# One attention-and-experts kernel: the shift row stored in row order, the first routing block's sums computed inside the last head, band loads moved ahead in the routing queue

## The reference

```python
x = x + attn(layernorm(x)); x = x + ffn(layernorm(x))
# attn: A = softmax(Q K^T / 4);  out = (0.6 * A + 0.4 * L) @ V;  out @ Wo.T + bo
#       L: a band, non-zero for |q - t| <= 3, rows normalised
# ffn:  rh = gelu(x @ rW1 + rb1);  p = softmax(rh @ rW2 + rb2);  top 2 of 4 experts
#       out = sum over the two experts e of p_e * (gelu(x @ We1[e] + be1[e]) @ We2[e] + be2[e])
```

## Time and profile before

| | us |
|---|---|
| median of 3 runs | 1982.28 |
| lowest, highest | 1981.71, 1989.45 |
| the profiled execution | 1984.26 |
| its span | 1982.5 |
| PE busy | 1915.1 |
| DVE busy | 1641.4 |
| ACT busy | 1342.0 |
| POOL busy | 370.3 |

### The profile page before, as it was taken

One profiled execution on the slowest core, in us unless ns is written; L12 is line 12 of the kernel. 1 busy time (PEld: TensorE's weight loads), 2 busy tenths in 40 slices (PEclk: granted clock), 3 DMA queues, 4 the chain that ended last, 5 costly groups with the idle time before them and its releaser, 6 DMA issues. The chain is left out here.

```text
span 1982.5 us, 40867 instructions
## 1 busy us (share of the span) xinstructions
PE 1915.1 (97%) x16092; PEld 1008.3 (51%) x16092; DVE 1641.4 (83%) x2123; ACT 1342.0 (68%) x2390; POOL 370.3 (19%) x380
## 2 busy tenths in 40 slices
PE   7999999999999999999999999999789899999997
PEld 3543333333333333333333333333477799999997
DVE  6799999999999999999999999994257665655554
ACT  3348888888888888888888888888434522232332
POOL 1362010101001100110010101010015632232233
PEclk9999999999999999999999999999889999999999
DMA  7954456545654565455545565453235777788884
GB/s 261 251 105 85 96 107 111 96 86 113 113 97 86 110 110 101 88 110 108 105 88 109 101 103 93 86 112 72 66 100 171 268 237 247 240 255 306 259 274 115
DMA packets 135341, 279.58 MB, mean 141 GB/s; under 512 B 45152, under 2 KB 75872, under 8 KB 128480
## 3 DMA queue, kind: packets, MB, share of 16 engines
q1 hardware_dynamic: 122000, 259.17, 53.0%
q0 software_dynamic: 13152, 17.83, 4.7%
HBM read 215.93 MB, written 79.06 MB: 149 GB/s over the span
## 5 line engine op out<-in xcount | busy, mean ns | idle before, releaser
L633 DVE TENSOR_REDUCE part_max<-psum 128x1 f32<-128x1024 f32 x1024 | 1244.8, 1221 | 29.4 <-PE psum L733 19.9
L691 ACT ACTIVATE probs<-psum 128x512 f32<-128x512 f32 x2048 | 1111.3, 596 | 157.9 <-PE psum L743 116.1
L743 PE MATMUL psum<-score_q,score_k 50*128 50x512 f32 x2048 | 746.1, 446 | 5.9 <-issue 5.4
L733 PE MATMUL psum<-max_k,max_q 48*128 48x512 f32 x2048 | 737.7, 449 | 1.0 <-DVE part_max L633 1.0
L755 PE MATMUL psum<-probs,v_ones 128*32 128x256 f32 x8192 | 654.1, 391 | 9.4 <-ACT heads_sb L697 9.0
L743 PEld LDWEIGHTS psum<-score_q,score_k 50*128 50x128 f32 x2048 | 304.9, 185 | 427.6 <-ACT probs L691 373.9
L755 PEld LDWEIGHTS psum<-probs,v_ones 128*32 128x32 f32 x8192 | 162.1, 107 | 383.8 <-ACT probs L691 194.9
L733 PEld LDWEIGHTS psum<-max_k,max_q 48*128 48x128 f32 x2048 | 294.1, 185 | 13.4 <-issue 7.0
L1150 ACT ACTIVATE x_sb<-psum,x_sb 128x512 f32<-128x512 f32 (+1 forms) x160 | 101.5, 635 | 253.9 <-PE psum L1546 253.9
L1565 PE MATMUL psum<-w,h_hi 128*128 128x256 f32 x1120 | 203.0, 280 | 0.0
L1565 PEld LDWEIGHTS psum<-w,h_hi 128*128 128x128 f32 x1120 | 179.4, 189 | 10.3 <-DVE h_lo L1361 0.2
(11 more groups left out here) (177 smaller groups left out, 1291.1 us busy)
## 6 DMA issues: line engine op xcount, KB each, us to landing
w<-w_split SPq DMA_DIRECT2D x40, 2048.0 KB, 8.4
max_q<-qk_pieces SPq DMA_DIRECT2D x192, 128.0 KB, 7.3
score_k<-qk_pieces SPq DMA_DIRECT2D x192, 128.0 KB, 4.6
xs<-in_pads SPq DMA_DIRECT2D x33, 528.0 KB, 4.6
qk_pieces<-pieces SPq DMA_DIRECT2D x32, 512.0 KB, 4.7
w_split<-w_pair SPq DMA_DIRECT2D x32, 512.0 KB, 5.2
max_k<-qk_pieces SPq DMA_DIRECT2D x192, 64.0 KB, 7.8
score_q<-qk_pieces SPq DMA_DIRECT2D x192, 64.0 KB, 2.3
```

Of the source, the lines that this page charges most:

```text
L633: nc.vector.tensor_reduce(part_max[:, u, t, p:p + 1], ps_m[p].rearrange("q b f -> q (b f)"), axis=AXIS.X, op=ALU.max).then_inc(m_read, 1)
L691: nc.scalar.activation(probs[:, kb % PROBS, chunk * BLOCK:(chunk + 1) * BLOCK], bank_of(k, kb, c), ACT.Exp, scale=float(HD) ** -0.5).then_ ...
L733: last = nc.tensor.matmul(ps_m[p][:, h, :], max_q[u][rows, t * P:(t + 1) * P], max_k[u][rows, p * BLOCK:(p + 1) * BLOCK], start=True, stop ...
L743: nc.tensor.matmul(bank_of(k, kb, c), score_k[u][rows, kb * P:(kb + 1) * P], score_q[u][rows, part * BLOCK:(part + 1) * BLOCK], start=True ...
```

## The change

1. `load_shift` stores the transposed tile with four DMAs, one for each group of 32 partitions, into a DRAM tensor laid out as rows of 1024 tokens; two DMAs then load two whole rows each (4 KB a row).
2. The transpose of the shift on DVE stands between the two maxima reductions of key tile 11 and no longer behind both.
3. In the last head PE computes the banded part of block 0 after key tiles 1 and 2, and its projection in four pieces (one for each 128 tokens, two matmuls each) after key tiles 7 to 10, into banks 6 and 7. DVE runs `mix_heads`, the residual sum and the statistics of block 0 at the end of its attention list, ahead of the barrier. SP loads the head outputs of block 0 at the start of the last head, the band and the head outputs of block 1 at its end.
4. In the routing queue of SP the scaling of the last head is spread over three turns of the loop, each part behind the band load of its turn: the inverse is stored at `i` = 1, spread at `i` = 2, the scaled head stored at `i` = 3. POOL's product moves behind the power of block 2. DVE's wait for the constants stands ahead of the first copy of `ids`.

```diff
+FIRST_LOCAL, FIRST_HEADS = (1, 2), (7, 8, 9, 10)
...
-    SHIFT_DMAS = PIECES * ROW_TILES
+    SHIFT_DMAS = ROW_TILES
...
-            sp.dma_start(dram["shift"], shift_tok[:]).then_inc(shift_out, 16)
-            sp.wait_ge(shift_out, 16 * (n + 1))
-            from_tiles = dram["shift"].rearrange("(q c h t) i -> h c t q i", q=P // QUAD, c=PIECES, h=ROW_TILES)
+            for q in range(P // QUAD):
+                sp.dma_start(dram["shift"][:, q, :], shift_tok[QUAD * q:QUAD * (q + 1), :]).then_inc(shift_out, 16)
+            sp.wait_ge(shift_out, 16 * P // QUAD * (n + 1))
+            rows = dram["shift"].rearrange("(c h t) q i -> h c (t q i)", c=PIECES, h=ROW_TILES)
             for h in range(ROW_TILES):
-                for c in range(PIECES):
-                    row = h * ROW_TILE + STACK + c
-                    sp.dma_start(score_q[u][row:row + 1, :].bitcast(F32).rearrange(
-                        "o (t q i) -> o t q i", q=P // QUAD, i=QUAD), from_tiles[h, c:c + 1]).then_inc(shift_in[u], 16)
+                row = h * ROW_TILE + STACK
+                sp.dma_start(score_q[u][row:row + PIECES, :].bitcast(F32), rows[h]).then_inc(shift_in[u], 16)
...
+            if last:
+                sp.wait_ge(o_out, 16 * BPS * (HEADS + 2))
+                load_heads(sp, dram, keep, 0, keep["heads_in"][0])
...
         by_head(body)
-        sp.wait_ge(o_out, 16 * BPS * (NHEADS + 1))
-        for i in range(2):
-            load_heads(sp, dram, keep, i, keep["heads_in"][i])
+        sp.wait_ge(keep["a_ready"][KD - 1], 1)
+        sp.dma_start(keep["band"][:], dram["band"][1]).then_inc(keep["band_in"], 16)
+        load_heads(sp, dram, keep, 1, keep["heads_in"][1])
...
         by_head(body)
+        mix_heads(nc, dve, keep, 0)
+        add_residual(nc, dve, keep, 0, ps_m[1])
...
                 values(n, kb, u, 1)
+                if last and kb in FIRST_LOCAL:
+                    m = FIRST_LOCAL.index(kb)
+                    pe.wait_ge(keep["band_in"], 16)
+                    pe.wait_ge(m_read, 2 * ST * NHEADS)
+                    local_values(nc, keep, psum[:, 4 + m, :], 0, m).then_inc(keep["a_ready"][m], 1)
+                if last and kb in FIRST_HEADS:
+                    t = FIRST_HEADS.index(kb)
+                    for m in range(KD):
+                        pe.wait_ge(keep["a_copied"][m], 1)
+                    done = project_heads(nc, keep, ps_m[1], t)
+                    if t == BT - 1:
+                        done.then_inc(keep["o_ready"], 1)
...
         for i in range(1, BLOCKS):
-            load_band(i)
+            if i > 1:
+                load_band(i)
             if i + 1 < BLOCKS:
                 sp.wait_ge(a_copied[KD - 1], i)
-                if i + 1 == HALF:
+                if i == 2:
+                    sp.wait_ge(inv_out, 16 * (NHEADS + 1))
+                    spread_inverse(sp, dram, keep, inv_in)
+                if i == 3:
+                    sp.wait_ge(scaled, NHEADS + 1)
+                    store_head(sp, dram, keep, (NHEADS + 1) % 2, NHEADS, o_out)
                     sp.wait_ge(o_out, 16 * BPS * (NHEADS + 2))
                 load_heads(sp, dram, keep, i + 1, heads_in[(i + 1) % 2])
             store_residual(i - 1)
             if i == 1:
                 sp.wait_ge(inv_ready, NHEADS + 1)
                 store_inverse(sp, dram, keep, inv_out)
-                sp.wait_ge(inv_out, 16 * (NHEADS + 1))
-                spread_inverse(sp, dram, keep, inv_in)
-                sp.wait_ge(scaled, NHEADS + 1)
-                store_head(sp, dram, keep, (NHEADS + 1) % 2, NHEADS, o_out)
...
-        projection(0)
         heads(1)
```

More of the change, by code:

```diff
@@ L628, in _, with maxima @@
     def _(dve):
-        def maxima(g, t, u):
+        def maxima(g, t, u, between=None):
             for p in range(2):
+                if p == 1 and between is not None:
+                    between()
                 dve.wait_ge(m_ready, 2 * g + p + 1)
@@ L670, in body @@
                 ahead = kb + LOOK - ST
+                turn = (lambda: transpose_shift(n + 1, shift_in[u], h + 1)) if kb == SHIFT_AT and not last else None
                 if not isinstance(n, int) or n + 1 + ahead // ST < NHEADS:
-                    maxima(ST * (n + 1) + ahead, ahead % ST, (u + 1 + ahead // ST) % 2)
+                    maxima(ST * (n + 1) + ahead, ahead % ST, (u + 1 + ahead // ST) % 2, turn)
+                elif turn is not None:
+                    turn()
                 if kb == INVERT_AT:
@@ L1398, in _ @@
         nc.vector.reciprocal(keep["inv_tok"][:], keep["sum_tok"][:]).then_inc(inv_ready, 1)
-        mix(1)
+        mix_heads(nc, dve, keep, 1)
         for i in range(BLOCKS):
@@ L1416, in _ @@
             if i + 2 < BLOCKS:
-                mix(i + 2)
+                mix_heads(nc, dve, keep, i + 2)
         weigh(BLOCKS - 2)
@@ L1465, in projection @@
             for t in range(BT):
-                for k in range(KD):
-                    last = nc.tensor.matmul(ps_w[:, t // 2, (t % 2) * DIM:(t % 2 + 1) * DIM],
-                                            attnT[:, k, t * P:(t + 1) * P], w_o[:, k, :],
-                                            start=k == 0, stop=k == KD - 1)
+                last = project_heads(nc, keep, ps_w, t)
             last.then_inc(o_ready, 1)
```

87 lines of the change are left out of this document (46 added, 41 removed).

## The result

The changed kernel takes 1965.72 us (median of 4 runs, 1960.27 to 1966.79), the kernel before, on the same chip, 1983.14 (4 runs, 1981.71 to 1989.45). The ratio is 0.9904, with a 95% interval of 0.9889 to 0.9918: about 19 us faster. Forecast were 1958.2 and a range of 1951 to 1968.

The account below looks back on a forecast made before the run. PE, busy nearly all the span, loses time waiting in the passage to routing and for the shift in heads. Gains of 19.6 + 4.5 = 24.1 us took 1984.26 to 1960.2, less 1.98 to the median: 1958.2, range 1951 to 1968.

Parts of the forecast that it names:

- The passage to routing: From attention to router(0) on PE: router(0) starts at 1429.8 against 1449.38, 19.6 us gained, range 16.5 to 26.0.
- The last head: Last attention head: added banded halves and projection stand in the limiting chain and lengthen it by 6.35 us, bounds 0 to 6.35.
- rival 2: Last head hides its additions in PE's room outside the chain: 6.35 us come back, 1951.9; chance 0.08.
- The shift: First-score waits in the attention heads: new layout and earlier transpose gain 4.5 us, bounds 0 and 5.4.
- the layout alone gains 0.2: Shift's store and load path in a slow head: 7.2 us instead of 7.4 from the row-order layout without the earlier transpose.
- From the profiled execution to the median: Whole kernel: the profiled execution of 1984.26 lies 1.98 us above the median, so 1960.2 becomes 1958.2.
- The prediction's estimate from the Trainium skill: Shift's path through DRAM: 5.7 us with about 2.0 us fixed cost per DMA, no shorter than before.
- what the mark gains the end gains: From router(0) to the end: PE is full and the experts follow, so router(0)'s 19.6 us reach the end.
- 1 (the shift gains nothing): Shift in the heads: the earlier store lands later or two-row loads are slow; 19.6 us remain, 1962.7; chance 0.14.
- 4 (the stores in a row make every head wait): Shift in 31 heads: four stores land one after another, 8.3 us of path gives back 16 us; chance 0.04.
- 3 (the wait moves to the band of block 4): Routing: block 4's band comes late, giving back 1 to 4 us, half clock up to 3 more, about 1964; chance 0.11.
- 5: Start of routing: unmoved constants and sums hold the routing block as long as before, 1978 or so; chance 0.03.

Follow-up runs that it names:

- the second execution: The changed kernel, unchanged, profiled a second time; span 1963.9 us, standing for the median.
- the first trace: The changed kernel's first profiled execution, its fastest: 1960.27 us, span 1958.5 us.
- e7: Kernel before with only routing's DMA queue order changed (bands first, scaling of the last head spread later, POOL's product one block later); 1971.67 us, ratio 0.9926.
- e8: Changed kernel with the shift's part and routing's queue order put back, leaving block 0's work in the last head and the moved addresses; 1991.06 us, ratio 1.0025.
- e11: Changed kernel with all old addresses, the last head's six insertions put into two (key tiles 1 and 8); 1958.97 us, ratio 0.9849.
- e4: Kernel before with only the shift stored by quarters in row order and loaded as whole rows, transpose and addresses as before; 1977.06 us, ratio 0.9948.
- e1: Kernel before with only the four routing tiles allocated ahead of the weights, moving what lies behind by 4256 bytes; 1991.5 us, ratio 1.0033.
- e6: Kernel before with only the shift's transpose moved between the two reductions of its unit; 1981.94 us, ratio 0.9970.
- e9: Changed kernel with the four routing tiles laid above all others, so every other tile has its old address; 1958.87 us, ratio 0.9850.
- e2: Changed kernel with 32 unused bytes per partition behind the four moved tiles, restoring the remainder by 64; 1964.69 us, ratio 0.9891.
- e5: Changed kernel with 96 unused bytes behind the moved tiles and 32 ahead of routing's own, restoring the remainder by 128; 1962.23 us, ratio 0.9872.

## Why the prediction came out as it did

The forecast of 1958 missed the median by 7.5 us inside its range, and one term is as large as that: the expert stage, which stood in the sum with nothing. The other terms' errors nearly cancel, which is luck: by the second execution the heads gave 3.9 us more than forecast, and the last head 0.7, the passage 0.9, the stretch to the first expert tile 0.6 and the step from the profiled execution to the median 2.0 us less. In order:

- *The passage to routing.* Right in its chain and nearly in its size. The path from barrier to router(0), forecast as 14.9 us, was 14.75 in the first trace and 1423.00 − 1407.19 = 15.8 in the second, where the granted clock stayed at 0.50 for about 7 us behind PE's idle time before the transposes, and for 3 to 4 us in the first, though the idle time was shorter in the second (2.79 against 3.04 us); the forecast had this among its bounds (up to 3.1). That the band wait goes and only a wait of 1.2 us comes in its place was tested by itself (e7), and that the rest of the gain adds to that by e8. What the wait for the bands cost in clock, some 2 us in the heads behind it, the forecast had in its path as 2.63 at full clock.
- *The last head.* The chain exponential, score, values, score was the limit: each added microsecond was paid, and rival 2 (they hide) is out. The size was 7.1 and not 6.35: the six insertions cost 0.77 us beyond their matmuls, 0.13 each, and e11 shows that this goes with their number. I had priced the matmuls as in routing, where they stand in longer rows.
- *The shift.* Mis-sized: 4.5 forecast, 7.0 measured (e4). Two causes. The step "the layout alone gains 0.2" was wrong: the path up to the end of the last load's issue got 1.0 us shorter in an ordinary head and 1.4 in a late one. In the ordinary head the four stores delay the loads by the 1.3 us that were forecast, but the two loads take 0.52 us to issue where the four took 2.81, 2.3 us less, and the sum had 1.7 for that. In the late head the stores cost only 0.9. And 5.4 us of waits is what one execution showed, no upper bound: others with the old store and transpose show 5.0 (e8), 6.6 (e7) and 7.3 (e1), and a wait can be followed by half clock. The transpose, which I credited with most of the gain, is the weaker part: alone it took 1.2 us off the waits (e6), and beside the row order nothing is left for it.
- *From the profiled execution to the median.* The forecast took off 1.98 us, because the profiled execution of the kernel before lay that much above the median of three. The medians of 9 to 26 executions are 1984.0 to 1985.7 us, so 1984.26 was an ordinary one and there was nothing to take off.
- *The prediction's estimate from the Trainium skill* ("DMA: Bandwidth & Descriptors", section "Anatomy of one DMA — SWDGE (gpsimd) path") came to a path no shorter than before. Its figure of 2.0 us is given there for transfers that GpSimd issues, and these go out on SP's queue; e4 decides: the path is shorter.
- *The expert stage.* The step that failed stands ahead of all others: "what the mark gains the end gains", said of router(0), since from there on a block follows another with PE full. PE was indeed full, and just for that reason each matmul that starts a little later costs time. The change moves four small tiles ahead of the weights, and with them the expert weights by 4256 bytes; e1 and e9 show that the move costs 7.2 us there and about 0.14 us for each routing block. The allocations stand in the change itself, and the sum had no term for them.
- *In the other direction,* the first profiled execution had fast heads, 3.9 us that the second one doesn't have; its other three times, 1965.2 to 1966.8, are like the second's. Had I compared only the profiled executions, the sum would have looked perfect (−24.0 for a forecast of −24.1), from errors of 7 us in both directions. The table's columns for the two executions keep them apart.
- *Rivals.* 1 (the shift gains nothing) and 4 (the stores in a row make every head wait) are out by e4. 3 (the wait moves to the band of block 4) came true in small: 0.5 us of wait in the first trace, none in the second, 1.2 in e7, where 1 to 4 were named. 5 is out by the passage.

The Trainium skill ("SBUF — State Buffer", section "Who interferes with whom") says that only the port pair shared by GpSimd and VectorE contends, and that PE has two read ports of its own, independent of each other. By that alone a tile's address would be worth nothing to PE. The measurement decides: 7.2 us for the same instructions in the same order (e1 against before, e9 against after).

Open is the mechanism. The remainder by 64 has no effect (e2), the remainder by 128 gives back 2.9 of 7.2 us (e5); the rest may hang on a larger boundary or on the distance of two operands, and was not tried. Open too is why every second head takes 39.68 us in one execution and 39.96 in all others, and the others 39.74 or 39.86.

## What to carry to other kernels

A change that moves a tile in memory is a change to every stage that reads what lies behind it: where PE is full, put new tiles behind all others, or run the layout by itself first (one run, e1, showed 7.5 us that no row of the profile before had pointed to). Before adding up a forecast against one profiled execution, compare stage by stage by marks and look at a second execution; a total that agrees can hold two errors of opposite sign. Work put into a chain in which two engines take turns is paid in full, and here 0.13 to 0.17 us more for each insertion, so put it in few pieces, or, as with the constants, move what only waits for a queue.

## What the runs showed that was not expected

- Matmuls of one kernel at the same granted clock of 1.00 take 1.8% longer (405.28 against 398.24 us over the expert tiles) when their operands lie 4256 bytes further on; in the attention the same move shows no loss.
- A single wait of PE of 1.3 us in the middle of the attention was followed, some 2 us later, by 13 us at half clock although PE was busy again all that time (e8, 1210 to 1230: 0.50 and 0.83); that cost 5.6 us in one head. In e1 1.7 us of wait were followed by 7 us at half clock. A wait of 1.26 us in e7 was followed by none.
- Four stores of 4 KB, issued one after another, and two loads of 8 KB are a faster way across than one store of 16 KB and four loads of 4 KB: 3.24 against 4.26 us up to the end of the last load's issue in an ordinary head, 4.65 against 6.01 in a late one.
